# Setting the causal triangle to zero on GpSimd, once per four heads, in place of mask matmuls

## The reference

```
x = x + attn_a(layernorm(x));  x = x + ffn(layernorm(x))
x = x + attn_b(layernorm(x));  x = x + ffn(layernorm(x))

# attn_b, per head
att = einsum('bhqd,bhkd->bhqk', q, k) / sqrt(hd)
att = where(tril(ones(T, T)), att, -inf)
att = sparsemax(att)            # max(z - tau, 0), tau so that a row sums to 1
y   = einsum('bhqk,bhkd->bhqd', att, v)
```

## Time and profile before

| | |
|---|---|
| median of 3 runs | 748.38 us (747.91 to 749.77) |
| the profiled execution, its own time | 748.38 us |
| its span in the trace | 745.4 us |
| busy share of the span: PE, PEld | 89%, 66% |
| DVE, ACT, POOL | 62%, 51%, 64% |
| mean granted TensorE clock, as a share of full | 0.946 |

### The profile page before, as it was taken

The page is one execution under the profiler, slowest core; times in us unless marked ns, Lnnn a source line. Parts: engine busy times, 40 slices in busy tenths (PEclk is TensorE's granted clock), DMA queues, the critical chain, the costliest instruction groups (busy, mean ns, idle before and its releaser), DMA issues.

```text
span 745.4 us, 18579 instructions
## 1 busy us (share of the span) xinstructions
PE 667.0 (89%) x6534; PEld 489.1 (66%) x6534; DVE 458.7 (62%) x1322; ACT 382.0 (51%) x929; POOL 474.1 (64%) x887
## 2 busy tenths in 40 slices
PE   2578988998888998889999999999999999999985
PEld 2335545665656665656677778777777888888664
DVE  1476666665666766666666666666665666766321
ACT  1004545555555545556665555545555655555651
POOL 7554457566866666877767676676567666653333
PEclk9567999899999999999999999999999999999996
DMA  8534344244344344343544433432234333430000
GB/s 253 150 82 117 93 124 118 67 106 117 102 113 106 85 100 117 98 116 96 121 112 106 115 99 82 101 91 73 60 84 107 103 95 101 102 102 11 17 9 17
DMA packets 64349, 72.08 MB, mean 97 GB/s; under 512 B 10748, under 2 KB 57916, under 8 KB 59644
## 3 DMA queue, kind: packets, MB, share of 16 engines
q1 hardware_dynamic: 64252, 70.84, 37.7%
HBM read 46.60 MB, written 23.33 MB: 94 GB/s over the span
## 4 chain that ended last, share of the span: by engine, by line
PE 46%; POOL 26%; issue 16%; DVE 4%; SPq 3%; DMA 2%; ACT 1%; POOLq 0%; ACTq 0%; DVEq 0%
PE banks L1357 9%; PE banks L1323 5%; PE banks L1342 5%; PE banks L1306 4%; PE banks L1297 3%; POOL qk L856 3%; PE banks L1324 3%; PE banks L1344 3%; POOL qk_parts L860 3%; PE banks L1298 3%; POOL qk L850 3%; POOL f_xhat L840 3%; PE banks L1279 2%; PE banks L1339 2%; PE banks L1320 2%
## 5 line engine op out<-in xcount | busy, mean ns | idle before, releaser
L1171 ACT ACTIVATE probs_t<-banks 128x512 f32<-128x512 f32 (+1 forms) x512 | 273.9, 555 | 201.1 <-PE banks L1339 112.6
L1008 DVE TENSOR_REDUCE neg_shift<-banks 128x2 f32<-128x512 f32 x256 | 172.0, 684 | 111.2 <-PE banks L1320 110.6
L1013 DVE MAX8 top<-banks 128x8 f32<-128x128 f32 x256 | 75.2, 294 | 110.0 <-PE banks L1324 109.0
L1357 PE MATMUL banks<-probs_t,v_ext 128*32 128x256 f32 (+1 forms) x2048 | 130.0, 373 | 0.5 <-ACT probs_t L1171 0.5
L1320 PE MATMUL banks<-k_stack,q_stack 72*128 72x256 bf16 x512 | 107.0, 296 | 11.3 <-DVE neg_shift L1008 5.4
L906 POOL TENSOR_TENSOR hidden<-up_tanh,gate_half 128x256 f32<-128x256 f32 x96 | 69.5, 727 | 62.5 <-DVE up_tanh L1047 62.4
L1339 PE MATMUL banks<-q_stack,k_stack 75*128 75x256 bf16 x512 | 102.7, 283 | 6.6 <-ACT probs_t L1171 6.3
L1014 DVE MAX8 top<-banks 128x8 f32<-128x256 f32 x256 | 106.2, 415 | 0.0
L1323 PE MATMUL banks<-k_stack,q_stack 72*128 72x128 bf16 (+1 forms) x512 | 100.5, 248 | 4.9 <-DVE top L1014 3.9
L1342 PE MATMUL banks<-q_stack,k_stack 75*128 75x256 bf16 (+1 forms) x512 | 99.1, 247 | 2.2 <-ACT probs_t L1171 2.2
L1324 PE MATMUL banks<-mask_b,ident_b 128*128 128x128 bf16 x512 | 99.8, 219 | 0.0
(11 more groups left out here) (90 smaller groups left out, 1132.7 us busy)
## 6 DMA issues: line engine op xcount, KB each, us to landing
q_stack<-q_image SPq DMA_DIRECT2D x96, 192.0 KB
k_stack<-k_image SPq DMA_DIRECT2D x96, 192.0 KB
q_image<-qk_parts SPq DMA_DIRECT2D x32, 192.0 KB, 2.1
k_image<-qk_parts SPq DMA_DIRECT2D x32, 192.0 KB, 2.4
q_image<-qk_parts SPq DMA_DIRECT2D x32, 128.0 KB, 2.1
o_image<-out_t SPq DMA_DIRECT2D x32, 128.0 KB, 2.4
out_compact<-o_image SPq DMA_DIRECT2D x64, 32.0 KB, 3.0
rdenominators<-r_image SPq DMA_DIRECT2D x16, 128.0 KB, 2.4
```

Source lines behind the costliest of these rows:

```text
L1008: dve.tensor_reduce(m.nm[:, n % STACKS, h, :], scores.rearrange("p (q k) -> p q k", q=TT), AX.X, ALU.max, negate=True).then_inc(reduced, 1)
L1171: act.activation(m.pt[:, g % 2, i, 0:size], shifted_banks[:, j % 2, 0:size], ACT.Exp if is_soft(n) else ACT.Relu, scale=SCALE if is_soft(n ...
L1357: ins = pe.matmul(out_bank[32 * i:32 * i + 32, at + skip:at + T], v_windows(v, kt)[:, Q * g + i, :], m.pt[:, g % 2, i, kt * T:(kt + 1) * T ...
```

## The change

The two mask matmuls in the second pass of the plain items are gone. Instead `clear_future` on GpSimd sets the triangle of the finished probabilities to zero, with one AFFINE_SELECT for the four heads of a group: on each partition 8 blocks (4 heads, 2 key blocks) of 128 columns, in place in `m.pt`. It keeps a value where column minus partition is 0 or more, and writes 0.0 elsewhere. `pv` of a plain item waits for that selection and no longer for the ACTIVATEs. `m.pt` gets a third group. `pv` and `take_out` of the plain items move two steps later (35 to 37, 49 to 51). To make room in SBUF some tiles share storage: the integer weights lie in `x2` until they are scaled, and two scratch tiles of the exact fallback path lie in the rotary tiles. The mask matmuls of the first pass stay.

```diff
+P_GROUPS = 3
...
-    m.wf_int = sb("wf_int", [P, 3 * HIDDEN], I32)
+    m.wf_int = m.x2[:, 0:3 * NC_H, :].rearrange("p c d -> p (c d)").bitcast(I32)
...
-    m.pt = sb("probs_t", [P, 2, Q, 2 * T])
+    m.pt = sb("probs_t", [P, P_GROUPS, Q, 2 * T])
...
-          pass2=30, pv=35, take_out=49, store_out=50, ...
+          pass2=30, pv=35, pv_plain=37, take_out=49, take_out_plain=51, store_out=50, ...
...
+            def clear_future(n, g):
+
+                pool.wait_ge(probs_ready, n * H + Q * g + Q)
+                blocks = m.pt[:, (n * Q + g) % P_GROUPS, :, :].rearrange("p i (k x) -> p i k x", k=TT)[:, :, :, 0:P]
+                pool.affine_select(blocks, blocks, pattern=[[0, Q], [0, TT], [1, P]], compare_op=ALU.is_ge, fill=0.0,
+                                   base=0, channel_multiplier=-1).then_inc(causal_ready, 1)
...
             for step in range(FIRST_STEP, LAST_STEP):
+                n, j = divmod(step - AT["pass2"] - Q, H)
+                if B <= n < ITEMS and j % Q == 0:
+                    clear_future(n, j // Q)
...
             def probs(n, j):
                 g, i = divmod(j, Q)
-                wait(act, pv_done, n * Q + g - 1)
+                wait(act, pv_done, n * Q + g + 1 - P_GROUPS)
...
-                        pe.matmul(shifted[:, first:first + T - kt * P], k, m.qs[r][0:SHIFTED, j, kt * P:T],
-                                  start=True, stop=True)
-                        ins = pe.matmul(shifted[:, first:first + P], m.ident_b[:, :], m.maskT_b[:, :],
-                                        start=False, stop=True, skip_group_check=True)
+                        ins = pe.matmul(shifted[:, first:first + T - kt * P], k, m.qs[r][0:SHIFTED, j, kt * P:T],
+                                        start=True, stop=True)
...
             def pv(n, g):
-                pe.wait_ge(probs_ready, n * H + Q * g + Q)
+                if is_soft(n):
+                    pe.wait_ge(probs_ready, n * H + Q * g + Q)
+                else:
+                    pe.wait_ge(causal_ready, (n - B) * Q + g + 1)
```

More of the change, by code:

```diff
@@ L1167, in probs @@
                 g, i = divmod(j, Q)
[L1168 removed]
+                wait(act, pv_done, n * Q + g + 1 - P_GROUPS)
                 act.wait_ge(shifted_ready, n * H + j + 1)
                 size = 2 * T if is_soft(n) else T + P
[L1171 removed]
+                act.activation(m.pt[:, (n * Q + g) % P_GROUPS, i, 0:size], shifted_banks[:, j % 2, 0:size],
                                ACT.Exp if is_soft(n) else ACT.Relu,
@@ L1199, in _ @@
             for step in range(FIRST_STEP, LAST_STEP):
-                if (n := due(step, "take_out")) is not None:
+                if (n := due(step, "take_out")) is not None and is_soft(n):
+                    take_out(n)
+                if (n := due(step, "take_out_plain")) is not None and not is_soft(n):
                     take_out(n)
@@ L1400, in _ @@
                     pass2(n, j)
-                n, g = divmod(step - AT["pv"], H)
-                if 0 <= n < ITEMS and g % Q == 0:
-                    if n == 0 and g == 0:
-                        pe.wait_ge(bias_ready, 2)
-                    pv(n, g // Q)
+                for soft, what in ((True, "pv"), (False, "pv_plain")):
+                    n, g = divmod(step - AT[what], H)
+                    if 0 <= n < ITEMS and is_soft(n) == soft and g % Q == 0:
+                        if n == 0 and g == 0:
+                            pe.wait_ge(bias_ready, 2)
+                        pv(n, g // Q)
                 if step == 16 * ITEMS + 7:
```

9 lines of the change are left out of this document (4 added, 5 removed).

## The result

The changed kernel takes 768.14 us, the median of 4 runs (763.6 to 771.68); the kernel before took 748.14 us beside it, also over 4 runs (746.75 to 749.77). The ratio is 1.024, with a 95% interval of 1.0189 to 1.0291. It is slower. The forecast was 732 us and faster; 768 lies in the range, but on the side that I held for the less likely one. The profiled execution took 771.68 us, the longest of the four; its span is 768.8.

The account below looks back on a forecast made before the run. TensorE bounds the plain half, GpSimd after the change; 12.1 + 4.3 + 3.7 + 1.5 - 1.3 = 20.3 us, less 4 for coupling, gives 748.4 - 16.3 = 732.1 us; 8-in-10 range 721 to 785 us.

Parts of the forecast that it names:

- rival 2: GpSimd becomes the bound at the two-input price, 2.4 us per selection: about 796 us; chance 0.17, of which 0.03 far up.
- The price of the selection: On GpSimd, 64 selections of 1024 columns each cost 1.05 us, taken from the cast row.
- TensorE's ceiling: Removed masks free TensorE of 15.4, 7.4, 3.7 and 2.7 us by stage, 29.2 in all, the most the change can bring.
- GpSimd's own queue: In the plain stages, time less waits plus selections: 133.1 + 34 x 1.05 = 168.8 us, and 57.8 + 16 x 1.05 = 74.6.
- The stage as the larger of two queues: First two plain stages last as long as GpSimd's queue, now slower than TensorE's: 12.1 and 4.3 us shorter, less 4 for coupling.
- the new wait: Selection's wait at the head of GpSimd's queue, some two us at worst, is over on arrival while GpSimd runs behind TensorE.
- My sign for a mis-sized coupling: Selection near 1.05 us but time not below 742: TensorE's waits must lie at turned thresholds, feed-forward products or `pv`.
- Rival 5: Less busy TensorE in the first plain stage gets clock 0.95: 5.4 us more, 737.5 us; inside the main forecast's 0.48.
- Rival 1: GpSimd becomes the bound in the plain half, from 1.41 or 1.32 us per selection; 755 us at 1.58; chance 0.19.
- `pv` and its copy out: Moving both two steps later in the plain items costs nothing: same work at another place of a full queue.
- The last two stages: Third stage: TensorE's 3.7 us come off whole; fourth: 1.5 come off, and the chain at the end adds 1.3.

Follow-up runs that it names:

- e3: Changed kernel with the selection at its place and with its wait, but over 8 columns of each block and not 128: 742.23 us.
- e1: Changed kernel without the selection, so neither masks nor selection; later pv and third group stay: 731.89 us.
- e2: Changed kernel with full-size selections reading a constant and writing a scratch tile, so they wait for no engine and pv waits for ScalarE's ACTIVATEs: 747.63 us.
- e15: Changed kernel with the selection cut to 8 columns per block, then a full-size one on its own tile that nobody waits for: 769.93 us.
- e8: Changed kernel with neither masks nor selection, and pv and copy out of plain items back at their old steps: 730.07 us.
- e5: Changed kernel with pv and copy out of the plain items two steps earlier, at their old places (35 and 49): 819.78 us.
- e18: Changed kernel with masks kept up to item 24 and all four selections only from item 25 on: 745.05 us.
- e9: Changed kernel with the first and last group's selections moved behind the splits of thresholds and of q and k, by one and two steps: 769.97 us.

## Why the prediction was wrong, step by step

The range held 768 us by luck. Its upper part was there for a selection of up to 2.2 us (rival 2), and the selection cost 1.10. What follows is about the forecast of 732.

**The price of the selection: right.** 1.05 us forecast, 1.10 measured (70.6 us for 64). e3 gives its slope: (1102 - 302) / 960 = 0.833 ns a column, the memset's 0.834. The Trainium skill's rule ("GPSIMD Engine Reference", section 3.1) of 1.8 cycles per element at best, by which my estimate was 1.54 us, doesn't hold here: the row has 1.10.

**TensorE's ceiling: right in the steady stage, wrong in the mixed one.** 71.5 us forecast, 71.15 in e1. But the 15.4 us of the mixed stage were taken off in full because TensorE was busy 96% there, and e1 lost 4.4. I wrote that what is taken from its queue "comes off the time, as long as nobody else is late"; others were late as soon as TensorE was faster. In e1 it waits for VectorE's eight largest in the plain items (4.6 us), GpSimd's normalised output of the first block (2.6) and others, and 4.8 us of the masks' work (15.4 less 10.6) went to a slower clock in two items.

**GpSimd's own queue: right.** 140.8 us before in the mixed stage, cut at the item, and 33 selections of 1.05 make 175.5; after has 174.9. In the steady stage 74.6 forecast, 76.8 in e2 and in after.

**The stage as the larger of two queues: this is the step that failed.** I forecast 165.5 us for TensorE and 168.8 for GpSimd and took the larger plus 4 us. That holds only in e2's steady items, where the selection waits for nobody, and in two of e15's. It fails in the mixed stage of e2 already: 198.69 us, where the larger queue was 175.5. I also wrote of the new wait that it "is over when it gets there". It isn't: GpSimd still waits 37.1 us in the mixed stage of after and 12.6 in the steady one, 19.5 and 8.0 of them at the selection, because the engines that it waits for are themselves waiting for it. A steady item is GpSimd's queue plus the waits in it: 19.2 + 1.4. At full clock that is 20.56 us, slower than before's 19.71, and already the wrong sign. Beyond the larger queue (175.5 and 74.6 us) the two stages of after are 36.5 and 14.8 us longer, clock included, where I had allowed 4. My sign for a mis-sized coupling named TensorE's waits at the turned thresholds, the feed-forward products or `pv`; in the mixed stage `pv` has 4.0 us, and the rest stands mostly at the norms and the normalised output (13.1 us) and at VectorE's eight largest (5.2).

**The clock: mechanism right, size wrong.** Rival 5 expected a lower clock from a less busy TensorE and priced it at 5.4 us. In the steady stage alone it took 7.2, and one item at 0.85 costs 2.7 us; in the mixed stage TensorE's 1846 matmuls are busy 11.6 us longer than in e1. I priced it on TensorE's queue and let GpSimd cover the first part. But GpSimd waits for TensorE too, so nothing covers it: the steady item at 0.85 is longer by all of the 2.68 us that TensorE is busy longer.

**Rival 1** named the right engine with the wrong reason: it needed c above 1.32 to 1.41 us. The loss came at 1.10.

**`pv` and its copy out: at nothing, and right within what the times show** (e8), though with selections their move is needed (e5). **The last two stages:** -3.7 and -0.2 forecast; -3.15 and -2.15 measured.

What stays open: how the mixed stage's 25 us over e1 divide between waits and clock. TensorE's busy time says 11.6 and its idle time 13.7, but a slower clock lengthens waits, and the clock falls behind gaps, and no run holds one of them still.

## What to carry to other kernels

The larger of two queues is a lower bound of a stage and no forecast. A new instruction that waits for a second engine, while that engine waits for results from further down the same queue, closes a ring. It cost 1.2 us per item even where GpSimd had room (e3), and waits stayed where its queue was nearly the whole item. So follow the chain out of the new instruction and back to its own engine (here 2.2 us from the selection through `pv` and VectorE to the norm) and compare it with what that engine has to do meanwhile (1.7 us). Before moving work off the busiest engine run the removal alone: it gives the ceiling (here 18 to 23 us of the 29 that the timeline suggested). Moving only a quarter or half of it, near places where the other engine waited, kept 9 to 12 us.

## What was not expected of the hardware

- TensorE's granted clock fell to 0.50 right behind two waits of 1.33 and 1.15 us close to each other, although it had been busy 1.90 of the 2.00 us before and was fully busy after. It did so in three of after's four steady items, for some 3.4 to 6.7 us, and not in the fourth, with the same two waits; and in three of e18's. In e9 TensorE has two waits in each steady item too (1.15 and 1.38 us), but 11 us apart, and the clock was 1.00 in all four; its first item:

```profile
610.67 0.86 PE L1375 MATMUL banks<-probs_t,v_ext 128*32 128x256 f32 x16 [1.15 <-POOL probs_t L913]
...
621.61 0.86 PE L1375 MATMUL banks<-probs_t,v_ext 128*32 128x256 f32 x16 [1.38 <-POOL probs_t L913]
```

  A single wait can be enough: in e15's last steady item the clock fell to 0.50 behind one of 1.74 us (the item's mean is 0.85), while its second and third item had the same wait and stayed at 1.00. So these runs show that a fall stands behind waits of one to two microseconds, and not what decides which wait brings one.
- A selection costs the same in place on fresh data and from a constant tile: 1102 and 1094 ns for 1024 columns. Of this 0.25 us doesn't grow with the columns (302 ns at 64 columns less 64 x 0.833).
